# One block for projection and attention: attention's first steps between the projection's last ones

## The reference, cut to what matters

```
h = layernorm(x) * (1 + ca) + sa
q, k, val = (proj(W) for W in (Wq, Wk, Wv))              # (2, 16, 2048, 16) each
R_hat = (1 + exp(vv)) / (1 + exp(vv - wv * R))           # R[i, j] = |i - j|, per head
scores = relu(einsum('bhqd,bhkd->bhqk', q, k)) * R_hat   # causal, -inf above the diagonal
attn = softmax(scores / sqrt(16))
ctx = einsum('bhqk,bhkd->bhqd', attn, val)
x = x + ga * (ctx @ Wo + bo)
```

## Time and profile before

| what | value |
|---|---|
| median of 3 runs | 1547.54 us (1546.9 to 1552.03) |
| the profiled execution | 1547.5 us, of which 1545.6 us are the profile's span |
| PE, DVE, ACT, POOL busy | 94%, 78%, 69%, 60% of the span |
| chain that ended last | PE 75%, DVE 6%, ACT 3%, issue 3% |

### The profile page before, as it was taken

One profiled execution on the slowest core, in us unless ns is written; L12 is line 12 of the kernel. 1 busy time (PEld: TensorE's weight loads), 2 busy tenths in 40 slices (PEclk: granted clock), 3 DMA queues, 4 the chain that ended last, 5 costly groups with the idle time before them and its releaser, 6 DMA issues.

```text
span 1545.6 us, 43427 instructions
## 1 busy us (share of the span) xinstructions
PE 1455.7 (94%) x16150; PEld 1141.3 (74%) x16150; DVE 1201.0 (78%) x3707; ACT 1065.1 (69%) x2294; POOL 930.2 (60%) x1542
## 2 busy tenths in 40 slices
PE   6896999999999999999999999999997758999997
PEld 4552888888888888888888888888885547676675
DVE  6645999999999999999999999999966696223222
ACT  3444888988888888888898888888874771211211
POOL 3334787788777777788777887788793002334322
PEclk9996999999999999999999999999998857999999
DMA  6343223222222223223222223222344334334431
GB/s 224 123 155 128 62 65 93 75 67 63 77 88 72 64 66 93 75 67 89 77 89 72 64 66 96 73 66 63 115 140 135 91 116 137 100 89 122 131 78 22
DMA packets 90035, 142.50 MB, mean 92 GB/s; under 512 B 18032, under 2 KB 69632, under 8 KB 85728
## 3 DMA queue, kind: packets, MB, share of 16 engines
q1 hardware_dynamic: 82058, 128.70, 26.9%
q0 software_dynamic: 6464, 9.29, 3.2%
q10 hardware_dynamic: 1302, 1.74, 0.3%
HBM read 109.56 MB, written 30.15 MB: 90 GB/s over the span
## 4 chain that ended last, share of the span: by engine, by line
PE 75%; DVE 6%; ACT 3%; issue 3%; SPq 2%; DMA 2%; POOLq 0%; POOL 0%; DVEq 0%; ACTq 0%
PE turn_ps L827 26%; PE pv_ps L842 16%; PE score_ps L816 15%; PE bank L1285 7%; PE bank L1295 7%; DVE region_x L895 2%; SPq L169 1%; ACT region_c L862 1%; ACT region_x L867 1%; SPq L126 1%; PE bank L1197 1%; PE bank L1136 1%; DMA heads_out<-region_o 1%; DVE region_p L1463 1%; DMA inverse<-compact 1%
## 5 line engine op out<-in xcount | busy, mean ns | idle before, releaser
L816 PE MATMUL score_ps<-region_s 128*128 128x512 bf16 (+3 forms) x1280 | 405.9, 354 | 15.6 <-DVEq L880 10.8
L827 PE MATMUL turn_ps<-ident,region_a 128*128 128x128 f32 x2048 | 328.7, 274 | 2.9
L827 PE MATMUL turn_ps<-ident,region_x 128*128 128x128 f32 x2048 | 331.1, 274 | 0.0
L930 POOL TENSOR_SCALAR region_x<-region_x,maxima 128x1664 f32<-128x1664 f32 (+3 forms) x128 | 202.3, 1581 | 175.8 <-ACT region_x L867 172.4
L827 PEld LDWEIGHTS turn_ps<-ident,region_a 128*128 128x128 f32 x2048 | 255.0, 141 | 41.8 <-ACT region_c L862 10.2
L895 DVE CUSTOM_DVE_ANT_0 region_x<-score_ps,region_t,maxima 128x512 f32<-128x512 f32 (+1 forms) x416 | 269.0, 699 | 16.1 <-PE score_ps L816 16.1
L827 PEld LDWEIGHTS turn_ps<-ident,region_x 128*128 128x128 f32 x2048 | 253.7, 141 | 28.2 <-ACT region_o L862 6.5
L862 ACT ACTIVATE region_p<-turn_ps 128x512 f32<-128x512 f32 x384 | 224.1, 608 | 69.0 <-PE turn_ps L827 69.0
L862 ACT ACTIVATE region_o<-turn_ps 128x512 f32<-128x512 f32 x448 | 266.5, 618 | 0.2
L867 ACT ACTIVATE region_x<-region_x 128x384 f32<-128x384 f32 (+1 forms) x512 | 247.3, 508 | 3.9 <-DVE maxima L895 3.3
L895 DVE CUSTOM_DVE_ANT_0 region_a<-score_ps,region_t,maxima 128x512 f32<-128x512 f32 (+1 forms) x352 | 230.6, 694 | 18.0 <-PE score_ps L816 17.9
(11 more groups left out here) (220 smaller groups left out, 2452.5 us busy)
## 6 DMA issues: line engine op xcount, KB each, us to landing
region_t<-factor_rows SPq DMA_DIRECT2D x32, 1024.0 KB
region_x<-in_fc_t SPq DMA_DIRECT2D x16, 1024.0 KB, 8.5
region_s<-q_split SPq DMA_DIRECT2D x64, 192.0 KB
region_s<-k_split SPq DMA_DIRECT2D x64, 192.0 KB
q_split<-region_o SPq DMA_DIRECT2D x16, 384.0 KB, 2.7
k_split<-region_t SPq DMA_DIRECT2D x16, 384.0 KB, 2.6
heads_out<-region_o SPq DMA_DIRECT2D x254, 17.0 KB
region_x<-in_x SPq DMA_DIRECT2D x4, 1024.0 KB, 15.5
```

Of the source, the lines that this page charges most:

```text
L816: nc.tensor.matmul(score_ps[:, j % SB, 0:(hi - lo) * P], stacks[:, b, 0, t * P:(t + 1) * P], stacks[:, b, 1, lo * P:hi * P], start=True, s ...
L827: last = nc.tensor.transpose(turn_ps[:, (h * NR + j) % TB, q * P:(q + 1) * P], rows[t][:, k * P:(k + 1) * P], ident[:, :])
L930: nc.gpsimd.tensor_scalar(row, row, maxima[:, 4, n:n + 1], 1.0, ALU.add, ALU.mult).then_inc(shifted_pool, 1)
```

## The change

Attention's plan is started inside the projection's block; the block's end between the two is gone.

- `attention` no longer opens a block. It returns for each engine a function `emit` (the same steps as before) and a class `Opening`, which hands out the plan's steps with a time below 0 piece by piece; `over_heads(emit, opening)` then hands out the rest.
- In the last two groups (g = 6 and 7) each engine runs the steps of the opening between its projection steps. `reached` translates a place in the projection into a time of the plan: 1.72 for a unit, 3.45 for a value step, so that the 19 rounds are spread over what follows the second unit of group 6.
- The seven loads of head 0, batch 0 are issued behind stores 17 to 23 instead of 20 to 26, and with them the wait for stores 0 to 15 and for the factors' stores is moved.
- The seven loads of batch 1 are issued when all stores have landed and TensorE has made its last value step.
- The eight PSUM banks are shared between the two. Up to slot 27 the scores have three banks instead of four. Slots 0 to 2 wait for the last uses of their banks in the projection, the fourth bank waits for the last `remainder`, and the first turn for that and for the last copy of the values. `ht` holds two groups instead of eight, some small buffers move into `region_c`, and waits guard the buffers that now overlap.

```diff
+            def reached(g, units, values):
+                if g < NG - 2:
+                    return -math.inf
+                time = (g - (NG - 2)) * BESIDE / 2 + units * UNIT + values * VALUE
+                return (time - 2 * UNIT) * LEAD / (BESIDE - 2 * UNIT) - LEAD
+            def beside(u):
+                return reached(u // 4, u % 4 + 2, 0) if u % 4 < 3 else reached(u // 4 + 1, 1, 0)
 ...
-                    if u == 4 * (NG // B) + SPLITS:
+                    if u == 4 * (NG // B) + 1:
 ...
-                    part = u - 4 * (NG // B) - SPLITS
+                    part = u - 4 * (NG // B) - 1
                     if 0 <= part < HEAD_LOADS:
                         load_part(sp, 0, 0, part)
                 for i in range(SPLITS):
-                    sp.wait_ge(st_split[i], 16 * 4 * NG // SPLITS)
+                    sp.wait_ge(st_split[i], ALL_SPLIT)
+                sp.wait_ge(val_mm, 2 * NG)
+                load_head(sp, 0, 1)
+                over_heads(emit, opening)
 ...
                     nc.gpsimd.tensor_tensor(parts[u % SPLITS][:, 2, :], ...).then_inc(part3, 1)
+                    opening.until(beside(u))
 ...
                     if u >= 1:
                         second(u - 1)
+                    if i < 3:
+                        opening.until(reached(g, i + 2, 0))
                 if g == NG - 1:
                     second(4 * NG - 1)
                 for i in range(2):
+                    opening.until(reached(g, 4, i + 1))
                     act.wait_ge(val_mm, 2 * g + i + 1)
 ...
                             remainder(u)
+                            opening.until(beside(u))
 ...
                         last.then_inc(proj_mm, 1)
+                        opening.until(reached(g, i + 1, 0) - 0.7)
 ...
                         last.then_inc(val_mm, 1)
+                        opening.until(reached(g, 4, i + 1) - 0.7)
 ...
-        attention(nc, locals())
+                over_heads(emit, opening)
 ...
+    score_ps = pbank[0:3] + [pbank[5]]
+    turn_ps = [pbank[3], pbank[4], pbank[6]]
+    early = [(t, what, j) for t, what, j in events if t < 0]
+    def bank_of(s):
+        return s % (SB - 1) if s < EARLY_SCORES else s % SB
+    class Opening:
+        def until(self, time):
+            while self.done < len(early) and early[self.done][0] < time:
+                _, what, j = early[self.done]
+                self.emit(what, j, 0)
+                self.done += 1
 ...
+                if s == 0:
+                    pe.wait_ge(ht0_done, NG)
+                if s == 1:
+                    pe.wait_ge(ht1_done, NG)
+                if s == 2:
+                    pe.wait_ge(gates_done, 2 * B)
+                if s == next(at for at in range(NS) if bank_of(at) == SB - 1):
+                    pe.wait_ge(rest1, 4 * NG)
+                pe.wait_ge(scaled, FREE_SCALED + freed_by(s) + 1)
 ...
+                if (h, j) == (0, 0):
+                    pe.wait_ge(rest1, 4 * NG)
+                    pe.wait_ge(val_done, 2 * NG)
```

More of the change, by code:

```diff
@@ L10 @@
+import math
 from contextlib import ExitStack
@@ L296, in _, with evacuate @@
                                             ALU.subtract).then_inc(part3, 1)
-            def evacuate(act, split, second, g):
+                    opening.until(beside(u))
+                over_heads(emit, opening)
+                for g in range(NG // B):
+                    add_bias(nc, pool, g)
+            def evacuate(act, split, second, opening, g):
                 for i in range(4):
@@ L488, in _ @@
                     remainder(u)
+                    opening.until(beside(u))
+                over_heads(emit, opening)
+                for g in range(NG // B):
+                    normalise(nc, dve, g)
             @block.tensor
@@ new lines, in over_heads, with sync_program, emit @@
+    def over_heads(emit, opening):
+        opening.until(1.0)
+        for t, what, j, h in order_of_all:
+            if t >= 0:
+                emit(what, j, h)
+    def sync_program(sp):
+        def emit(what, j, h):
+            if what == "load" and h < H - 1:
+                sp.wait_ge(scaled, h * NS + (FREE_SCALED + last_of[j] + 1))
+                load_head(sp, h + 1, j)
+            elif what == "dump":
+                quads = range(STREAMS // 2 if (h, j) == (H - 1, GROUPS - 1) else STREAMS)
+                dump(sp, pv_saved, h * GROUPS + (FREE_SAVED + j + 1), sums, h, j, quads, (firsts, seconds))
+            elif what == "x2":
+                sp.wait_ge(values_done[j // 2], H)
+                load_x2(sp, x, j)
+            elif what == "compact" and (h, j) != (H - 1, B - 1):
+                if h:
+                    sp.wait_ge(spread[j], 16 * h)
+                gather_sums(sp, h, j)
+            elif what == "spread" and (h, j) != (H - 1, B - 1):
+                spread_inverse(sp, h, j)
+                if (h, j) == (H // KC, 0):
+                    for g in range(NG // B):
+                        load_heads(sp, g, 0)
+                if (h, j) == (H - 1, 0):
+                    sp.wait_ge(scaled, h * NS + (FREE_SCALED + last_of[0] + 1))
+                    for g in range(NG // B):
+                        load_heads(sp, g, 1)
+                    sp.wait_ge(spread[j], 16 * H)
+                    for g in range(NG // B):
+                        for k in range(KC):
+                            load_inverse(sp, g, k)
+        return emit
@@ new lines, in tensor_program, with emit @@
+    def tensor_program(pe):
+        pe.sem_inc(turned, FREE_TURNED)
+        pe.sem_inc(pv_done, FREE_PV)
+        def emit(what, j, h):
+            if what == "score":
+                n, lo, hi = slots[j]
+                b, t = tiles[n]
+                if j == first_of[b]:
+                    pe.wait_ge(loaded[b], h * LOADS + LOADS)
+                s = h * NS + j
+                if s == 0:
[7 more added lines that the diff above has]
+                pe.wait_ge(scaled, FREE_SCALED + freed_by(s) + 1)
+                nc.tensor.matmul(score_ps[bank_of(s)][:, 0:(hi - lo) * P], stacks[:, b, 0, t * P:(t + 1) * P],
+                                 stacks[:, b, 1, lo * P:hi * P], start=True, stop=True).then_inc(score_done, 1)
+            elif what == "turn":
+                b = j // (NR // B)
+                if (h, j) == (0, 0):
+                    pe.wait_ge(rest1, 4 * NG)
+                    pe.wait_ge(val_done, 2 * NG)
+                if j % ROUNDS == 0:
+                    pe.wait_ge(masked, h * NTL + max(masked_to[number[b, block_of(j, q)[0]]] for q in range(STREAMS)))
+                pe.wait_ge(exp_done, h * NR + (FREE_EXP + j + 1 - TB))
+                for q in range(STREAMS):
+                    t, k, short = block_of(j, q)
+                    if short and k == 0:
+                        pe.wait_ge(masked, h * NTL + masked_to[number[b, t]])
+                    last = nc.tensor.transpose(turn_ps[(h * NR + j) % TB][:, q * P:(q + 1) * P],
+                                               rows[t][:, k * P:(k + 1) * P], ident[:, :])
+                last.then_inc(turned, 1)
+            elif what == "pv":
+                g = j // len(BATCHES)
+                b = g // 2
+                if j % len(BATCHES) == 0:
+                    pe.wait_ge(pv_saved, h * GROUPS + (FREE_SAVED + g))
+                    if g % 2 == 0:
+                        pe.wait_ge(values_done[b], h + 1)
+                pe.wait_ge(exp_done, h * NR + (FREE_EXP + batch_end[j] + 1))
+                for r in range(NR):
+                    if batch_of[r] == j:
+                        for q in range(STREAMS):
+                            t, k, short = block_of(r, q)
+                            last = nc.tensor.matmul(pv_ps[VW * q:VW * (q + 1), short, :], vblock[:, b, k, :],
+                                                    weight(r)[:, q * P:(q + 1) * P], start=(k == 0), stop=(k == t))
+                last.then_inc(pv_done, 1)
+        return emit
```

355 lines of the change are left out of this document (154 added, 201 removed).

## The result

The changed kernel takes 1558.84 us (median of seven runs, 1557.44 to 1562.84); the kernel before, 1549.83 us (seven runs). The ratio is 1.0057, 95% interval 1.0046 to 1.0068: slower by 9.0 us, clear of the interval. The forecast was 1554.4, the range 1542 to 1563. It stood on the 1547.54 us of three runs of the kernel before; against the median of seven it forecast 6.9 us more than before, and 9.0 were measured. The profiled execution took 1558.49 us with a span of 1556.5.

What follows compares the result with a forecast made beforehand. TensorE, busy 94% of the span, bounds the kernel, so the start of slot 40 moves the end; 5.7 us later there plus 1.2 for the clock is 6.9 on 1547.5, giving 1554.4 us, range 1542 to 1563.

Steps and rivals of the forecast that it cites:

- What would show it: Signs in the profile after: slot 0 near 115, last store near 145, some 10 us gap before slot 40, half clock behind both.
- Slot 0 at 115.0: Batch 1's opening aside, batch 0's first score waits for seven loads until 115.0 us, bounds 112 and 118; TensorE idles 10 us.
- Rival 3: TensorE's clock stays at 1.2 GHz through the opening; store 31 some 11 us later, 1565 us; chance 0.13.
- From slot 0 to `remainder(31)`, 25.6 us: DVE's path: 4.5 us to its start, 12.0 of opening work, 4.1 of remainders, 5.0 waiting for TensorE; `remainder(31)` at 140.6.
- From `remainder(31)` to the landing, 7.1 us: Projection's tail: remainder and second rounding 1.2 us, POOL behind by 2.0, its own part 1.15, store landing 2.7.
- Batch 1's loads, 22.4 us: Head 0's loads on three DMA engines, issued at 148.0 behind all stores, take 22.4 us as before and land at 170.4.
- Slot 40, +5.7: First score of batch 1: TensorE meets it at 160.4, waits 10 us for loads, starts at 170.5 instead of 164.8.
- The clock behind it, +1.2: Behind the wait at slot 40, 2 to 5 us at 1.2 GHz cost 1 to 2.5 us; 1.2 taken.
- The barrier that goes was under 0.5 us: Between store 31's landing and batch 1's first load, the removed barrier had cost under 0.5 us.
- rival 1: Pieces come sooner and cancel: slot 0 at 112, slot 40 at 165 to 166.5, total 1548 to 1551 us; chance 0.22.
- Rival 2: Batch 1's loads land within 13 us of issue, so the opening's gain is kept: 1538 to 1543 us; chance 0.09.
- The rule on DMA width: SP's DMAs use as many engines as divide the outermost dimension, lowest-numbered first: 3, 3 and 2; earlier issue doesn't widen them.

Runs made afterwards that it cites:

- the repeat whose clock didn't fall at 43 us: Second repeat of the changed kernel, nothing altered, to see whether the clock's fall in group 0 comes again; slot 40 started at 171.59 us.
- The wide loads: Changed kernel with q_split and k_split in DRAM as (D, 3, tokens), so q and k loads and stores have 16 or more outermost; 1539.13 us, ratio 0.9923.

## Why the prediction was right, by its steps

**The mechanism.** Slot 0 waits for batch 0's loads, everything behind it up to store 31 moves, batch 1's loads go out late, slot 40 waits, and the clock falls behind both gaps. Each link is in the profile after, and shortening batch 1's loads alone gave back 9.1 us. The sign came as forecast, and so did the marks named in "What would show it", the gaps longer than I had them. The sizes, one by one:

- *Slot 0 at 115.0*: 118.12; 116.48 in the repeat whose clock didn't fall at 43 us. So 1.5 us were my working of the loads' queue, and the rest came from further up. It lies at the upper bound of 118, and would be 0.1 us beyond it.
- *TensorE at 1.2 GHz on resuming*: yes, 3.4 us of it, and then 2.4 GHz for all of the opening. Rival 3, which kept it down, is refuted.
- *From slot 0 to `remainder(31)`, 25.6 us*: 23.2 (118.12 to 141.29). The first remainder came 4.4 us behind slot 0, as worked out (4.5). With 12.0 and 4.1 us of DVE's work as counted, 2.7 are left for the waits on TensorE, where I had 5.0.
- *From `remainder(31)` to the landing, 7.1 us*: 8.3 (141.29 to 149.6). POOL was further behind than 2 us, as its order of time shows: a shift of 1.98 us, the third parts 29 and 30 (1.38 and 1.15 us) and small steps stand in front of part 31, at 145.77.

```profile
140.93 1.98 POOL L1014 TENSOR_SCALAR region_x<-region_x,maxima 128x1792 f32<-128x1792 f32 x1
142.89 1.38 POOL L319 TENSOR_TENSOR region_o<-region_c,region_o 128x512 bf16<-128x512 f32 x1
...
144.49 1.15 POOL L319 TENSOR_TENSOR region_t<-region_c,region_t 128x512 bf16<-128x512 f32 x1
...
145.77 1.15 POOL L319 TENSOR_TENSOR region_t<-region_c,region_t 128x512 bf16<-128x512 f32 x1
```

- *Store 31 landed at 147.7*: 149.6, the sum of these three (+3.1, -2.4, +1.2). *First turn at 148.4*: 149.73.
- *Batch 1's loads, 22.4 us*: 23.5 (149.69 to 173.2). TensorE meets slot 40 at 159.7, forecast at 160.4; that this is so near is luck, since the first turn came 1.3 us later than forecast and the way from there took 10.0 us and not 12.0, with the clock at 2.4 GHz all along. Its wait is 13.5 us where I had 10.
- *Slot 40, +5.7*: +8.45 in the pair of profiles, +8.1 in the means of three. This is the mis-sized term: batch 1's loads were issued 1.7 us later (149.69 for 148.0) and took 1.1 us longer than I had them.
- *The clock behind it, +1.2*: right. From slot 40 to the same turn it is 4.65, 4.87 and 4.63 us in the three profiles after and 3.29 us in all three before, so 1.3 to 1.6 us. The rows of the first pair, after and before:

```profile
177.89 0.27 PE L905 MATMUL pbank<-ident,region_a 128*128 128x128 f32 x1
```

```profile
168.08 0.27 PE L827 MATMUL turn_ps<-ident,region_a 128*128 128x128 f32 x1
```

  The working behind the term was rougher: the 91 records in 6.5 us that it names don't stand in the earlier trace rows (a window from 157.5 to 164.0 has 89), and they are of other work than the 19. Half clock cost 1.36 us in a stretch of 2.95, less than "half or more".

**Where it was wrong in substance.** "The barrier that goes was under 0.5 us": that was read on SP's queue alone. The block's end also held TensorE from the end of the value steps at 124.1 until 134.94, while store 31 landed; without it, and with nothing interleaved, the scores start at 126.53 and the kernel is 7.5 us faster (moved loads included). I had counted this gain only inside "the opening comes sooner", and so I could not see that one half of the change is a gain and the other a loss of 16.2 us (1558.84 - 1542.64).

**Rivals 1 and 2.** The cancelling of rival 1 didn't come: slot 0 was not at 112. Rival 2 named its own condition, loads landed within 13 us of issue, and 1538 to 1543 as the time. Its condition was false here. The wide loads met it with 10.3 us and gave 1539.13, with slot 0 at 112.67 and the first turn at 144.37, near what it had; but they also freed the stores from the narrow loads, so the agreement is no clean test of it.

**The rule on DMA width.** The share of 0.19 in the second gap is again 3 of 16 engines. The layout with 16 outermost took it to 0.91, and the packet counts fit 3, 2 and 16 engines exactly, in two edits of which one kept the DRAM layout. That bears out what the prediction cites from the Trainium skill ("DMA: Bandwidth & Descriptors", section "Why a DMA increments its semaphore by 16 and not by 1"). That the lowest-numbered engines are the ones used is not shown by these runs.

## What to carry to other kernels

Before work is merged across a barrier, list what each side must have landed at the seam, and follow a delayed last store to the loads that stand behind it in the queue: the work brought forward is paid for by what it pushes back. Price a barrier on every engine that it holds, each part of a change on its own, and ask of a load that is moved forward not only who waits for it but which stores will stand behind it. A load that is slow because of its shape is mended by its shape: here 10 us of overlap were only to be had once the loads were wide and early, and neither of the two was enough by itself.

## What the runs showed of the hardware

How many DMA engines a load used can be read off the packet count of the page: 2560 more small packets for 192 loads that were made wide, 240 more for the six of one head and batch, just what 3 and 2 engines against 16 give. Six narrow loads make stores of the same queue late that have nothing to do with them: with all loads of batch 0 behind one store, the split that needed store 18's buffer stood idle for 13.50 us. TensorE's clock fell to 1.2 GHz behind a wait of only 3.3 us at 43 us in some executions of one and the same kernel and not in others (eleven of thirteen profiles in all), which made group 0 some 1.7 us longer, so one pair of profiles can differ by that much without any cause in the code; only the repeats told that apart. Why an execution falls to one side or the other is open.
